# Attention and feed-forward block on one core: part of the softmax denominators summed on VectorE, the cosine product moved there, a new step table

## What is computed

```
q_rot, k_rot = rotate(q), rotate(k)
num  = exp(q_rot @ k_rot.T * scale)
den  = sum(exp(q @ k.T * scale), axis=-1)      # q, k not rotated, no mask
attn = where(causal, num / den, 0)
x = x + (attn @ v) @ Wout + bout
```

## Time and profile before

| | us |
|---|---|
| median of 3 runs | 1656.57 |
| lowest and highest | 1656.44, 1657.23 |
| profiled execution | 1656.43 |
| its span, first to last instruction | 1654.7 |

### The profile page before, as it was taken

The page is one execution under the profiler, slowest core; times in us unless marked ns, Lnnn a source line. Parts: engine busy times, 40 slices in busy tenths (PEclk is TensorE's granted clock), DMA queues, the critical chain, the costliest instruction groups (busy, mean ns, idle before and its releaser), DMA issues.

```text
span 1654.7 us, 25505 instructions
## 1 busy us (share of the span) xinstructions
PE 1483.4 (90%) x8226; PEld 572.7 (35%) x8226; DVE 851.1 (51%) x1961; ACT 1587.1 (96%) x2641; POOL 521.9 (32%) x863
## 2 busy tenths in 40 slices
PE   4888989999999989999899899989999999999986
PEld 2322333333333333333343343333333333333334
DVE  5334434765346653566445653566434665356416
ACT  2999999999999999999999999999999999999992
POOL 3324133432234322333332323334133432234310
PEclk8998999999999999999999999999999999999998
DMA  5532233331434313333234234333243421433300
GB/s 160 156 99 80 86 106 115 120 101 55 131 115 131 111 44 122 122 124 106 80 118 124 94 96 131 100 121 97 73 131 115 141 93 42 135 113 103 115 27 26
DMA packets 95389, 172.05 MB, mean 104 GB/s; under 512 B 15696, under 2 KB 82256, under 8 KB 83152
## 3 DMA queue, kind: packets, MB, share of 16 engines
q1 hardware_dynamic: 94656, 169.55, 32.7%
q10 hardware_dynamic: 592, 0.79, 0.2%
HBM read 111.55 MB, written 58.72 MB: 103 GB/s over the span
## 4 chain that ended last, share of the span: by engine, by line
ACT 88%; PE 6%; issue 4%; DVE 1%; DMA 1%; DVEq 0%; ACTq 0%; POOL 0%; SPq 0%; POOLq 0%
ACT scores L541 57%; ACT probs L551 27%; ACT probs L553 4%; PE scores L599 2%; PE y_ps L628 1%; PE side L638 1%; PE scores L606 1%; PE scores L657 0%; DMA x_in<-in_L_attn_x 0%; PE side L657 0%; PE scores L647 0%; PE scores L773 0%; ACTq L315 0%; PE scores L784 0%; DVEq L894 0%
## 5 line engine op out<-in xcount | busy, mean ns | idle before, releaser
L541 ACT ACTIVATE scores<-scores 128x1024 f32<-128x1024 f32 x1024 | 1067.6, 1122 | 16.8 <-PE scores L599 16.5
L599 PE MATMUL scores<-stack 96*128 96x512 bf16 x2048 | 585.3, 385 | 77.8 <-ACT scores L541 40.1
L551 ACT ACTIVATE probs<-scores 128x1024 f32<-128x1024 f32 x512 | 491.7, 1111 | 2.8 <-PE scores L606 1.7
L606 PE MATMUL scores<-stack 96*128 96x512 bf16 (+3 forms) x1536 | 335.0, 330 | 46.7 <-ACT scores L541 37.6
L438 POOL TENSOR_SCALAR_AFFINE_SELECT probs<-probs 128x256 f32<-128x256 f32 (+1 forms) x640 | 240.8, 403 | 387.7 <-ACT probs L551 219.0
L628 PE MATMUL y_ps<-probs,v_sb 128*32 128x512 f32 (+3 forms) x3072 | 331.8, 504 | 5.1 <-POOL probs L438 5.1
L599 PEld LDWEIGHTS scores<-stack 96*128 96x128 bf16 x2048 | 152.6, 97 | 486.1 <-ACT scores L541 209.9
L541 ACT ACTIVATION_READ_ACCUMULATOR scores<-scores 128x1 f32 x1024 | 300.5, 293 | 0.0
L448 POOL TENSOR_TENSOR parts<-rest,parts 128x512 bf16<-128x512 f32 x124 | 143.2, 1155 | 292.8 <-DVE parts L961 292.8
L606 PEld LDWEIGHTS scores<-stack 96*128 96x128 bf16 x1536 | 116.9, 98 | 300.1 <-ACT scores L541 154.5
L446 POOL TENSOR_TENSOR rot<-raw,cos_sb 128x512 f32<-128x512 f32 x62 | 89.3, 1440 | 390.2 <-DVEq L971 390.2
(11 more groups left out here) (141 smaller groups left out, 1062.0 us busy)
## 6 DMA issues: line engine op xcount, KB each, us to landing
stack<-qk_parts SPq DMA_DIRECT2D x756, 128.0 KB, 2.6
qk_parts<-parts SPq DMA_DIRECT2D x127, 384.0 KB, 2.6
out<-x_mid SPq DMA_DIRECT2D x32, 256.0 KB, 2.9
x_in<-in_L_attn_x SPq DMA_DIRECT2D x7, 1024.0 KB, 5.3
stack<-qk_parts SPq DMA_DIRECT2D x18, 64.0 KB, 2.3
x_in<-in_L_attn_x SPq DMA_DIRECT2D x2, 512.0 KB, 4.4
probs<-in_L_attn_Wqkv SPq DMA_DIRECT2D x1, 512.0 KB, 5.7
cos_sb<-in_cos SPq DMA_DIRECT2D x1, 512.0 KB, 6.5
```

The source lines that it names most:

```text
L541: nc.scalar.activation(src, src, ACT.Exp, scale=SCALE, accum_out=den[:, g % 2, i, j:j + 1]).then_inc(exp_done, 1)
L551: nc.scalar.activation(probs[:, chunk % 2, j, :], src, ACT.Exp, scale=SCALE).then_inc(exp_done, 1)
L599: mm = nc.tensor.matmul(tile[:, half * HALF:(half + 1) * HALF], q[:, j, i * P:(i + 1) * P], k[:, j, half * HALF:(half + 1) * HALF], start= ...
L606: mm = nc.tensor.matmul(tile[:, col:col + n], k[:, h, i * P:(i + 1) * P], q[:, h, q0:q0 + n], start=True, stop=True)
```

## The change

1. SUMMED names 188 of the 1024 den steps by their number among the den steps of a unit. Their exponential goes without accumulator into one of two new SBUF tiles of 128x1024 f32 (sum_tiles). VectorE adds the two halves of the tile with a scalar_tensor_tensor whose accumulator gives the row sum (sum_den), at three steps behind (SUM_LAG). ScalarE waits for the sum two before (SUM_SLOTS = 2). A drain stands ahead of each reciprocal.
2. The cosine product leaves GpSimd: VectorE makes it from PSUM. The raw half tile is copied into rest, the shuffle is made in the qk step, and the subtraction is in place. The tile raw is gone.
3. The tiles hidden, logits_t, gate, w1_now and w2_now share the space of turned and rest; raw of the first unit shares xn2t; ones is one column wide, and the count of routed tokens is made in one row.
4. All step tables are new: ORDER, PV_STEPS, TAKE_Y, RECIPROCALS, SIDE, STATS1, STATS2 from (1, 29) to (1, 25), COPY from (1, 43) to (1, 28), GAP, BRANCH_LAST. A pair is (group, step).

```diff
@@ -58,11 +58,11 @@
 MASKS_UNIT = sum(MASKS.values())
 
 
-ORDER = [5, (0,), 4, (1,), 3, (2,), 7, (3,), 6, (4,), 7]
-
-
-ORDER_FIRST = [16, (0,), 1, (1,), 1, (2,), 1, (3,), 1, (4,), 12]
-ORDER_LAST = [0, (0,), 4, (1,), 0, (2,), 7, (3,), 11, (4,), 10]
+ORDER = [5, (0,), 5, (1,), 4, (2,), 7, (3,), 4, (4,), 7]
+
+
+ORDER_FIRST = [14, (0,), 1, (1,), 3, (2,), 1, (3,), 3, (4,), 10]
+ORDER_LAST = [0, (0,), 5, (1,), 3, (2,), 2, (3,), 12, (4,), 10]
 
 
 def unit_steps(order, dens):
@@ -89,22 +89,46 @@
 def unit_of(b, g):
     return G if b == B - 1 and g == G - 1 else G + 1 if b == 0 and g == 0 else g
 
+SUM_SLOTS, SUM_LAG = 2, 3
+SUMMED = [
+    (3, 10, 12, 19, 22, 27, 28),
+    (8, 19, 21, 24),
+    (11, 13, 19, 21, 25, 26),
+    (0, 3, 8, 18, 23, 24, 28),
+    (7, 8, 22, 28),
+    (7, 11, 12, 15, 16, 21),
+]
+
+
+def summed_steps(steps, chosen):
+
+    dens = [s for s, x in enumerate(steps) if x[0] == "den"]
+    return {dens[d]: k for k, d in enumerate(chosen)}
+
+
+SUM_AT = [summed_steps(steps, chosen) for steps, chosen in zip(STEPS, SUMMED)]
+
+
+def sums_ahead(b, g):
+
+    return sum(len(SUM_AT[unit_of(n // G, n % G)]) for n in range(b * G + g))
+
 
 PIECES = [(0, 0), (0, 1), (1, 0), (1, 1), (2, 0), (2, 1), (2, 2), (3, 1), (3, 0), (3, 2), (4, 0), (4, 1)]
 PV_STEPS = [
-    (15, 17, 25, 27, 33, 35, 37, 40, 42, 43, 45, 48),
-    (11, 20, 24, 26, 28, 34, 37, 38, 43, 45, 48, 49),
-    (11, 20, 23, 27, 29, 33, 35, 37, 41, 43, 45, 48),
-    (13, 15, 19, 26, 30, 33, 39, 41, 46, 47, 48, 49),
-    (6, 9, 20, 21, 25, 29, 30, 31, 35, 44, 46, 48),
-    (21, 23, 26, 28, 31, 33, 35, 38, 40, 42, 45, 47),
+    (15, 18, 25, 30, 32, 34, 38, 39, 41, 43, 45, 47),
+    (10, 21, 25, 28, 29, 31, 36, 40, 44, 45, 46, 48),
+    (11, 20, 22, 26, 28, 32, 35, 39, 42, 46, 48, 49),
+    (16, 21, 24, 27, 29, 36, 38, 40, 44, 46, 47, 48),
+    (7, 12, 18, 22, 27, 30, 31, 32, 33, 37, 45, 49),
+    (20, 23, 25, 30, 31, 32, 34, 38, 41, 44, 46, 49),
 ]
 PV_AT = [dict(zip(steps, PIECES)) for steps in PV_STEPS]
 CHUNK_END = [(0, 1), (1, 1), (2, 2), (3, 2), (4, 1)]
 Y_FIRST, Y_LAST = [(0, 0), (3, 0)], [(3, 1), (4, 1)]
-TAKE_Y = [47, 42, 37, 42, 36, 39]
+TAKE_Y = [39, 40, 41, 36, 29, 49]
 LOW_LAG = 3
-RECIPROCALS = (32, 25, 16, 25)
+RECIPROCALS = (28, 31, 16, 24)
 
 
 
@@ -114,19 +138,20 @@
 
 
 SIDE = [
-    {0: ("v", 0), 4: ("qk", 0), 8: ("v", 1), 12: ("v", 2), 14: ("turn", 1), 20: ("qk", 2), 28: ("turn", 3),
-     30: ("v", 3), 35: ("norm", 0), 38: ("norm", 1)},
-    {0: ("qk", 0), 3: ("acc", 0), 5: ("turn", 1), 7: ("qk", 2), 15: ("acc", 1), 17: ("acc", 2),
-     21: ("turn", 3), 22: ("acc", 3), 30: ("t2", 0), 33: ("t2", 1), 34: ("t2", 2), 38: ("t2", 3),
-     40: ("route", 0), 44: ("ffn", 0), 47: ("route", 1)},
-    {0: ("qk", 0), 5: ("ffn", 1), 7: ("route", 2), 8: ("turn", 1), 13: ("qk", 2), 17: ("ffn", 2),
-     22: ("norm", 0), 23: ("turn", 3), 26: ("ffn", 3), 29: ("norm", 1), 32: ("acc", 0), 36: ("acc", 1),
-     39: ("acc", 2), 46: ("xt", 0), 48: ("xt", 1)},
-    {0: ("acc", 3), 1: ("xt", 2), 6: ("xt", 3), 8: ("qk", 0), 12: ("ffn", 4), 14: ("turn", 1), 20: ("ffn", 5),
-     23: ("qk", 2), 28: ("turn", 3), 35: ("ffn", 6), 38: ("ffn", 7)},
-    {0: ("acc", 3), 2: ("ffn", 4), 5: ("ffn", 5), 9: ("ffn", 6), 17: ("ffn", 7), 37: ("end", 0),
-     38: ("end", 1), 40: ("end", 2), 47: ("end", 3), 49: ("end", 4)},
-    {0: ("qk", 0), 4: ("v", 0), 8: ("turn", 1), 10: ("v", 1), 14: ("qk", 2), 18: ("v", 2), 22: ("turn", 3), 24: ("v", 3)},
+    {0: ("qk", 0), 4: ("v", 0), 8: ("v", 1), 12: ("v", 2), 20: ("turn", 1), 21: ("qk", 2), 27: ("turn", 3),
+     28: ("v", 3), 35: ("norm", 0), 37: ("norm", 1), 48: ("acc", 0)},
+    {0: ("qk", 0), 3: ("turn", 1), 5: ("qk", 2), 14: ("acc", 1), 19: ("acc", 2), 20: ("turn", 3),
+     23: ("acc", 3), 30: ("t2", 0), 32: ("t2", 1), 35: ("t2", 2), 37: ("t2", 3), 41: ("route", 0),
+     44: ("route", 1), 47: ("ffn", 0)},
+    {0: ("qk", 0), 4: ("ffn", 1), 8: ("route", 2), 11: ("turn", 1), 13: ("qk", 2), 18: ("ffn", 2),
+     23: ("norm", 0), 27: ("norm", 1), 28: ("turn", 3), 30: ("acc", 0), 33: ("acc", 1), 37: ("ffn", 3),
+     44: ("acc", 2), 47: ("xt", 0)},
+    {0: ("acc", 3), 2: ("xt", 1), 4: ("xt", 2), 6: ("xt", 3), 8: ("qk", 0), 12: ("ffn", 4), 19: ("ffn", 5),
+     21: ("turn", 1), 23: ("qk", 2), 25: ("turn", 3), 32: ("ffn", 6), 35: ("ffn", 7)},
+    {2: ("acc", 3), 9: ("ffn", 4), 11: ("ffn", 5), 13: ("ffn", 6), 16: ("ffn", 7), 35: ("end", 0),
+     38: ("end", 1), 40: ("end", 2), 46: ("end", 3), 49: ("end", 4)},
+    {1: ("qk", 0), 3: ("v", 0), 6: ("turn", 1), 8: ("v", 1), 12: ("qk", 2), 17: ("v", 2), 21: ("turn", 3),
+     28: ("v", 3)},
 ]
 IN_TWO = {("v", 0), ("v", 1), ("v", 2), ("v", 3), ("qk", 0), ("qk", 2)}
 FFN = [("up", 0), ("up", 1), ("down", 0), ("up", 2), ("down", 1), ("up", 3), ("down", 2), ("down", 3)]
@@ -137,13 +162,13 @@
              ("logits", 1), ("down", 3), ("logits_t", 0), ("up", 0), ("up", 1), ("logits", 0), ("down", 0),
              ("down", 1), ("routed", 0)]
 IN_LOOP = sum(kind == "end" for kind, _ in SIDE[G].values())
-RECIPROCALS_LAST = (5, 35)
-BRANCH_LAST = 28
+RECIPROCALS_LAST = (6, 34)
+BRANCH_LAST = 24
 TILES = {"v": 4, "xt": 4, "qk": 2 * G, "norm": 4, "acc": 8, "t2": 4, "route": 3, "ffn": 8, "gen": 12 * E}
-STATS2 = (1, 29)
-STATS1 = {(1, 49): 0, (2, 4): 1, (2, 11): 2, (2, 15): 3, (2, 45): 4}
-COPY = (1, 43)
-GAP = (1, 49)
+STATS2 = (1, 25)
+STATS1 = {(1, 46): 0, (1, 48): 1, (2, 12): 2, (2, 19): 3, (2, 42): 4}
+COPY = (1, 28)
+GAP = (2, 5)
 BRANCH = (3, 42)
 
 
@@ -179,6 +204,7 @@
 
         stack = sb("stack", [P, 2, 2, 2, HG * C], BF16)
         probs = sb("probs", [P, 2, HG, C])
+        sum_tiles = sb("sum_tiles", [P, SUM_SLOTS, C])
         x_in = sb("x_in", [P, NB, D])
         xn = sb("xn", [P, 2, 2, D])
         xnt = sb("xnt", [P, KC, C])
@@ -197,10 +223,9 @@
         sin_sb = sb("sin_sb", [P, C])
         bias = sb("bias", [P, D])
         ident = sb("ident", [P, P])
-        ones = sb("ones", [P, P])
+        ones = sb("ones", [P, 1])
         parts = sb("parts", [P, 2, PARTS, HALF], BF16)
         rest = sb("rest", [P, HALF])
-        raw = sb("raw", [P, HALF])
         rot = sb("rot", [P, HALF])
         turned = sb("turned", [P, HALF])
         den = sb("den", [P, 2, NB, HG])
@@ -211,9 +236,9 @@
         rstd = sb("rstd", [P, 2, NB])
         root = [sb(f"root{i}", [P, NB]) for i in range(3)]
         xn2t = sb("xn2t", [P, KC, C])
-        hidden = sb("hidden", [P, 2 * P])
+        hidden = turned[:, 0:2 * P]
         hidden2 = sb("hidden2", [P, 2, 2 * P])
-        logits_t = sb("logits_t", [P, 2 * P])
+        logits_t = turned[:, 0:2 * P]
         logits = sb("logits", [P, NB, E])
         top = sb("top", [P, NB, 8])
         gap = sb("gap", [P, NB])
@@ -222,9 +247,9 @@
         prob = sb("prob", [P, NB, E])
         routed = sb("routed", [1, 1])
         routed_i = sb("routed_i", [1, 1], I32)
-        gate = sb("gate", [P, 2 * P])
-        w1_now = sb("w1_now", [P, KC, F])
-        w2_now = sb("w2_now", [P, D])
+        gate = turned[:, 2 * P:4 * P]
+        w1_now = rest[:, 0:KC * F].rearrange("p (k f) -> p k f", k=KC)
+        w2_now = rest[:, KC * F:KC * F + D]
 
         scores = ps("scores", [P, RING, 2 * HALF])
         y_ps = ps("y_ps", [P, HALF])
@@ -251,6 +276,7 @@
         exp_done = sem("exp_done")
         masked = sem("masked")
         chunk_used = sem("chunk_used")
+        summed = sem("summed")
         y_ready = sem("y_ready")
         y_taken = sem("y_taken")
         spread_ready = sem("spread_ready")
@@ -275,7 +301,7 @@
         end_full = sem("end_full")
         end_taken = sem("end_taken")
 
-        raw_of = [raw[:, :], y_sb[:, 0, 0:HALF]]
+        raw_of = [xn2t[:, 0, 0:HALF], y_sb[:, 0, 0:HALF]]
         rot_of = [rot[:, :], y_sb[:, 0, HALF:C]]
         rest_of = [rest[:, :], y_sb[:, 1, 0:HALF]]
         turned_of = [turned[:, :], y_sb[:, 1, HALF:C]]
@@ -441,9 +467,6 @@
             def low_part(b, g, t):
 
 
-                if t % 2 == 0:
-                    pool.wait_ge(raw_ready, at(b, 8, 2 * g + t // 2 + 1))
-                    nc.gpsimd.tensor_tensor(rot[:, :], raw[:, :], cos_sb[:, t // 2 * HALF:(t // 2 + 1) * HALF], ALU.mult)
                 pool.wait_ge(middle_ready, at(b, 16, 4 * g + t + 1))
                 nc.gpsimd.tensor_tensor(parts[:, t % 2, 2, :], rest[:, :], parts[:, t % 2, 1, :], ALU.subtract
                                         ).then_inc(low_ready, 1)
@@ -538,6 +561,12 @@
                     _, j, i = step
                     if s == FIRST_DEN[unit_of(b, g)] and not (first and g < 2):
                         act.wait_ge(den_used, at(b, G, g - 1))
+                    if s in SUM_AT[unit_of(b, g)]:
+                        k = sums_ahead(b, g) + SUM_AT[unit_of(b, g)][s]
+                        if k >= SUM_SLOTS:
+                            act.wait_ge(summed, k - SUM_SLOTS + 1)
+                        nc.scalar.activation(sum_tiles[:, k % SUM_SLOTS, :], src, ACT.Exp, scale=SCALE).then_inc(exp_done, 1)
```

(28 more changed lines are left out.)

## The result

| | before | after |
|---|---|---|
| median (lowest to highest), us | 1656.9 (1656.4 to 1657.3), 4 runs | 1695.7 (1695.2 to 1696.5), 4 runs |
| ratio to before, 95% interval | | 1.0239 [1.0227, 1.0250] |
| profiled span, us; mean granted clock | 1654.7; 0.984 | 1693.8; 0.968 |

The changed kernel is slower by 39 us. The forecast of 1665 had the sign, but the result lies above the whole range (1630 to 1672).

The account below looks back on a forecast made before the run. ScalarE, busy 96% of the span, was taken to bound the kernel. 1656.4 - 24.0 (denominators without accumulator) + 32.2 (COPY blocking the root) = 1664.6, say 1665 us, slower; range 1630 to 1672.

Parts of the forecast that it names:

- The first term: On ScalarE, 188 denominators without accumulator take a numerator's pace, 0.9025 instead of 1.03 us each: 24.0 us saved.
- The collision: In unit 1, COPY on GpSimd blocks VectorE's second layernorm root for 4.4 us, in batches 1 to 7.
- The price of the block: ScalarE stands 4.6 us in unit 1 of each of batches 1 to 7: 32.2 us added.
- rival C: After each pause TensorE's clock falls, 1 us more in each of 7 batches, or late sums: 1672 to 1680; chance 0.06.
- The new step tables ... zero: Tiles and pieces moved by a few steps inside units cost zero, with -6 to +6 us kept for the range.
- VectorE's total: VectorE's busy time with the new sums and cosine products: 1008 us, or 1160 at the upper price of a sum.
- The waits of ScalarE for its sums: ScalarE waits for the sum two before; about four steps, 4 us, lie between, so nothing was added.
- A: In unit 1, root and COPY miss each other or the lock gives way: 1632.4 us (1629 to 1638); chance 0.27.
- B: The block in unit 1 comes, but ScalarE stands only 2 us a batch: 1646 us; chance 0.07.
- D: VectorE's sum is slow, a block of 1 us in 15 uses, and no collision: 1647 us; chance 0.03.

Follow-up runs that it names:

- number 3: Kernel before with only COPY moved from (1, 43) to (1, 28): 1699.4 us, ratio 1.0272.
- number 10: Also called copy_memset: changed kernel, COPY at (1, 28) replaced by a GpSimd memset that only writes, input and bias left out: 1649.2 us, one run.
- number 8: Changed kernel with its new tables, COPY back at (1, 43) and no summed step: 1669.2 us, ratio 1.0079.
- number 7: Changed code with the step tables of the kernel before and no summed step: 1658.1 us, ratio 1.0018.
- Number 6: Changed kernel with new tables, COPY at (1, 43), one sum of group 1 and pieces of groups 0 and 3 moved: 1646.5 us, ratio 0.9946.
- number 1: Changed kernel with only COPY put back from (1, 28) to (1, 43): 1661.5 us, ratio 1.0034.
- Number 9: Changed code, old tables in units 0 and 1, mended new ones in units 2 and 3, COPY at (1, 43): 1638.4 us, ratio 0.9898.
- numbers 1 and 4: The second of the two: changed code with all step tables of the kernel before, only the first unit's sums chosen anew: 1686.2 us, ratio 1.0194.
- number 5: Changed code with the tables of the kernel before and other summed steps in groups 1 and 2, 180 in all: 1651.3 us, ratio 0.9977.
- number 2: Changed kernel, COPY at (1, 28) but cut into eight additions of 128x256: 1688.3 us, ratio 1.0203.

## Why the prediction was wrong

**The first term was right.** -24.0 forecast, -23.9 found in the starts: a summed step has a numerator's pace, 0.904 us. No price of writing SBUF instead of PSUM shows: the ACTIVATEs last 1073 ns into sum_tiles and 1078 in place.

**The collision was right in place and kind.** COPY was forecast at 26 to 27.7 us of the unit and began at 26.55; the root's remainder was to wait 4.4 and one operation lasted 4.41; the first transpose was forecast at 33.6 to 34.4 and came at 33.74 (934.64 - 900.90). Numbers 3 and 10 show it from both sides: one line brings it into a kernel without the rest of the change, and taking GpSimd's reads away removes it. The Trainium skill, page "SBUF — State Buffer", section "Who interferes with whom", states that a VectorE instruction with two SBUF inputs contends with a GpSimd instruction that reads SBUF and not with one that only writes it; the traces of copy_memset (0.17 us) and of the changed kernel (4.41) agree.

**The price of the block was too small; this is the first step that failed.** I took 4.6 us a batch, "the short end" of 4.5 to 5.5, from a transpose-to-exponential time of 1.2 to 1.34. Measured were 6.7. From the transpose to the exponential it was 1.98 (934.64 to 936.62), since TensorE did this work at half its clock, and the two steps behind were late by 0.65 each for the same reason. With the durations of the earlier trace rows the exponential would have come at 33.74 + 1.34 = 35.1, 4.8 late instead of 5.4, and nothing behind it: 4.8, not 6.7. I had the row for this (half clock, ScalarE 80% busy), priced it at 1 us and put it into rival C, as something that might follow the pause. It followed it in seven batches of seven (for 6.8 us in six, 3.4 in one), and in number 3 as well. It belonged in the sum, for 2 us a batch, 13 in all. That the slow clock costs this is read off the durations and the idle times; no run had the pause without the slow clock, so its share is worked out, not isolated.

**"The new step tables ... zero" is the second step that failed.** With the sums in their places they cost some 16 us here: outside the block 36 us are late against 16 before, less the 3.9 of start and tail, and number 10 leaves 16.7. Without sums it is 11 (number 8 less number 7). Each of the two failed steps, 15 us and 16, was enough to carry 1665 past 1672. I had compared the tables by TensorE's total slack in a unit, 3 us. But late time arises at a step, where a list puts two things together. In unit 0 the low part of qk 2 (GpSimd, L471) and turn 3 (VectorE) moved next to the numerators' masks (timeline of the changed kernel):
```profile
876.88 1.53 POOL L471 TENSOR_TENSOR parts<-rest,parts 128x512 bf16<-128x512 f32 x1 [7.32 <-DVE parts L990]
...
878.38 4.33 POOL L464 TENSOR_SCALAR_AFFINE_SELECT probs<-probs 128x256 f32<-128x256 f32 x8
...
882.85 1.07 PE L657 MATMUL y_ps<-probs,v_sb 128*32 128x512 f32 x8 [0.89 <-POOL probs L464]
...
884.49 1.02 ACT L580 ACTIVATE probs<-scores 128x1024 f32<-128x1024 f32 x1 [0.69 <-PE scores L635]
```
GpSimd waits 7.32 us for the cast and only then comes to its masks, which by then are late for TensorE (0.89) and so for ScalarE (0.69). In unit 3 TensorE has a qk half, a piece and a numerator chunk within the same two steps, while numerators ask for scores every 0.9 us; ScalarE waits 0.71 there (at 1030.74). Number 6 takes the place in unit 3 half away, moves the one in unit 0 and frees the sum behind COPY: 15 us against number 1. Number 9, with the old tables in units 0 and 1, wins 23. No run changed one of these places alone.

**The smaller terms.** The sum lasts 691 ns at the median and its accumulator's read 82, 0.77 together where I took 0.8 (the source view of line 1020: least, median, longest ns):
```profile
L1020 DVE SCALAR_TENSOR_TENSOR sum_tiles<-sum_tiles x188: 672/691/1680, 47.2 to 1663.8; 128x512 f32<-128x512 f32 x188
L1020 DVE DVE_READ_ACCUMULATOR sum_tiles<-sum_tiles x188: 75/82/85, 48.2 to 1664.4; 128x1 f32 x188
```
VectorE's total came to 978 us, forecast 1008. The waits of ScalarE for its sums, which I put at nothing, did no visible harm in the changed kernel, though one pair, in the first unit, has two steps between and not four; the term failed once COPY was moved (numbers 1 and 4), where a sum is what COPY catches.

**The rivals.** A (no collision, 1632) fell with the 4.41 us row, B (a part, 2 us a batch, 1646) with ScalarE's 5.23. C was right in mechanism: the clock falls. Its total, 1672 to 1680, lacked the second microsecond a batch and the tables. D fell: the Trainium skill, page "Vector Engine (DVE) Microarchitecture Reference", section "7. Points that are easy to get wrong", says half throughput for this form; the 691 ns are what any two-input operation of 512 f32 takes here (0.69), so no halving shows, and the measurement decides. With the two failed steps at their measured size the sum is 1656.4 - 23.9 + 47 + 16 = 1695.5; the last term is what the trace leaves over, so that the sum closes proves nothing more.

## What stays open

Number 9 still has late steps (step 25 of unit 3, 0.49, and step 11 of unit 2), 1638.4 against the 1633 of the plain sum; what makes steps 25 and 30 of unit 0 late in number 6 wasn't looked for. Half-clock stretches also come some 30 us after the pause, in unit 2 of the changed kernel, and unit 2 of number 5 differs from batch to batch; what starts them wasn't tried.

## What to carry to other kernels

Before moving a long GpSimd operation that reads SBUF, list VectorE's operations at the new place that read SBUF. Held until its end were, however small, those with two inputs in SBUF and a tensor_scalar from SBUF; a copy from PSUM wasn't, nor one with the second input in PSUM (L1022 in batch 0 of the kernel before, 0.69 us beside COPY). What depends on a held one is late by that. If TensorE pauses for that, as here for 4.65 us, price the stretch behind the pause at half its clock too. And a faster step at the bounding engine gives back only what the lists of the other engines can follow: compare tables step by step, not by a unit's total slack.

## What the runs showed of the hardware that I had not expected

- An operation of 8 columns on VectorE was held for the whole remainder of GpSimd's 4.5 us, as forecast (4.41 us); so was one with a single input, 4.39 us (number 3), which I hadn't expected.
- Cutting GpSimd's operation into eight leaves the total of the block nearly as it was: pieces and root operations take turns, 0.6 us for each of VectorE's (number 2).
- GpSimd's memset of 128x2048 f32 (1.81 us) holds no two-input operation of the root (number 10).
- At the end of a 4.65 us pause TensorE's granted clock fell to 0.50, for 6.8 us; the same work before the change, without the pause, ran at 1.00.
